# Kernel of four transformer layers: first attention as a pipeline over single tiles, ternary weights quantized inside the third layer's attention

## The chip, the cores and the metric

The kernel runs on one core of a Trainium2 chip. The metric is the device time of one execution in microseconds; the median of three runs is used. A core has the engines TensorE (PE, with its weight loads as PEld), VectorE (DVE), ScalarE (ACT), GpSimd (POOL) and SyncE (SP), which here only issues DMAs. Each engine runs its own list of instructions, and they meet at semaphores.

## What is computed

Four layers on 4096 tokens (64 sequences of 64) of width 256, float32. Each layer adds an attention and then a feed-forward part:

```
x = x + attention_l(layernorm(x), ctx, ...)
x = x + ffn_l(layernorm(x), ...)
```

The parts that the change touches are these. Layer 0's attention is over the 64 context rows of the same sequence, without projections, with a mask of keys:

```
scores  = xn @ ctx^T / 16, -1e30 where masked;  attn = softmax(scores)
out     = attn @ ctx, or 0 where a sequence has no valid key
```

Layer 0's feed-forward is a mixture of 32 experts (4 a token) and a shared expert, each `(silu(x w1) * (x w3)) w2`; layer 3's has 8 experts (2 a token) of width 176 and a shared one. Layer 1's feed-forward ("think") computes one vector for each sequence, from its last token, and adds `gate * vector` to each token before a layer norm. Layer 2's attention has 16 heads, a rotary part of the queries and keys, and weights that the kernel multiplies together beforehand. Layer 2's feed-forward is ternary:

```
quantize(w) = clip(round(w / (mean|w| + 1e-8)), -1, 1)
y = (silu(x Q(w1)^T) * (x Q(w2)^T)) Q(w3)^T          # w1, w2: 704 x 256, w3: 256 x 704
```

## The kernel before

x stays in SBUF (x_all) through the whole kernel, as 32 tiles of 128 tokens. The program is a row of stages, each with its own semaphores and buffers, which ends on all engines before the next begins. Between stages, finish_stats turns the mean and variance that each tile's last bn_stats left in bn_all into a mean and a reciprocal root, by three Newton steps on DVE (L195 to L210), and normalize (L219) uses them. The eight PSUM banks are c.bank[0] to c.bank[7].

stage_first loads x in four parts of eight tiles and takes their statistics (L262 to L271). stage_l0_attention then loads weights and masks, turns the masks into factors (keep, drop, any_valid, L454 to L456), and works in eight rounds of WIDE = 4 tiles. In a round each engine does each of its steps for four tiles before the next step. PE transposes xn and ctx (L226); makes key rows for the later layers' attentions (keys, L377, L380) and values and products with a Gram matrix (L384, L386) for them; makes the scores (L395); transposes prob (L401); and reads the context with it (L405). ACT copies out of PSUM and takes exponents (L441). DVE normalizes, multiplies the rotary key part with cosine and sine, scales and masks the scores and takes the maximum (L477 to L480), and adds the read to x with new statistics (L496, L498). POOL splits each context tile in three bfloat16 parts for layer 3 (L244 to L248), and adds the rotary products. SP loads a context tile to a slot when that slot's tile is done (x_done, L317), then stores the split parts (L324).

In the experts of layers 0 and 3, ACT takes the sigmoid of the gate half, DVE multiplies it with that half (L2942 in layer 3), and then by the other half to hid (L2944), which PE transposes.

In stage_l1_think tokens go in groups of four tiles. SP broadcasts each group's think rows from DRAM (L1321) into one of TH slots; POOL multiplies the gate with them (L1340) and does two more steps. After the second group's issue SP issues all seven weight loads for layer 2 (L1323 and following), some 4 MB, and the third group's rows come behind them. PE, ACT and DVE use these weights after their own last group.

stage_l2_attention works on two tiles in turn (LANES = 2, loops of pairs written with Fori). DVE's order for a tile is front (normalize, and a mask from three 64-wide operations, L1795 to L1798), maxima of the scores (L1818, L1820), sums of the exponents (L1825, L1826), rope of the next tile (L1809 to L1811, four times each), and back (L496, L498). POOL adds the rotated parts (L1667), PE makes queries (L1686), scores (L1721) and outputs (L1708).

stage_l2_ternary begins with a prelude in a block of its own: it loads the three raw weight matrices, takes their sums of absolute values (L1909 and its like), adds these over partitions by a matmul with ones, and quantizes each matrix with two comparisons and a subtraction (L1920 to L1922). Then come the tiles.

## Time and profile before

| | us |
|---|---|
| median of 3 runs | 2742.14 (2735.84 to 2747.07) |
| the profiled execution | 2754.47, span 2752.7 |
| load of x and its statistics | 0 to 22.0 |
| layer 0 attention | 22.4 to 225.1 |
| layer 0 experts (the last part) | 495 to 590 |
| layer 1 think | 777 to 954 |
| layer 2 attention | 959 to 1555 |
| quantization of the ternary weights | 1559.5 to 1586.6 |
| ternary feed-forward | 1587.2 to 1826 |
| layer 3 attention | 1832 to 2375 |
| layer 3 experts, with their gate | to 2752.7 |
| busy in the span: PE, DVE, POOL, ACT | 2011.5, 1745.9, 1170.6, 967.1 |

Times within the kernel are from the start of the profiled execution. In think, GpSimd's steps repeat every 8.3 us a group once the third has come (898.3, 905.9, 914.2, 922.5), and layer 2's precomputed weights follow on PE. In the rows of windows each engine's busy time has its number of instructions in brackets. "Idle before" in a row is the time that the engine stood still before the instruction, and "<-" names what released it. The granted clock is TensorE's as a share of full speed.

### The profile page before, as it was taken

Reading aid. Unit: us, or ns where it says so; the run is one execution under the profiler, and the core shown is the slowest. Engines: PE = TensorE matmul, PEld = TensorE weight load, DVE = VectorE, ACT = ScalarE, POOL = GpSimd, SP = SyncE. Lnnn points to the kernel's source line nnn. Section 1 sums busy time; section 2 is a strip of 40 time slices with the busy share of each in tenths; the row PEclk is TensorE's granted clock in tenths of the full one; section 3 lists DMA queues with packets and bytes.
Section 4 is the critical chain, followed back from the end, with each engine's and each line's share of the span. In section 5 each row is a group of like instructions: output and inputs, shape, how many; then the busy total and the mean of one; then the engine's idle time right before and its main releaser. Section 6 shows DMA issues by size and latency. Waiting matters only on the chain. (4 is left out here: it accounts for less than half of the span.)

```text
span 2752.7 us, 48931 instructions
## 1 busy us (share of the span) xinstructions
PE 2011.5 (73%) x17042; PEld 1511.4 (55%) x17074; DVE 1745.9 (63%) x3743; ACT 967.1 (35%) x2509; POOL 1170.6 (43%) x1482
## 2 busy tenths in 40 slices
PE   4776927536976077777777479959999999458995
PEld 3666826315855066666666356635666665135774
DVE  5554479324554878888888544457887885633446
ACT  2442201102423233333343122215666666222331
POOL 2430000462323745555555222335887887063331
PEclk9777965657988589999999789978999999778998
DMA  4224100561076100000000000024444441222336
GB/s 116 55 54 162 38 8 2 161 163 47 5 183 106 31 1 0 0 0 0 0 0 0 32 1 1 1 49 97 104 110 111 96 112 45 71 90 66 107 105 212
DMA packets 142050, 174.97 MB, mean 64 GB/s; under 512 B 30380, under 2 KB 123740, under 8 KB 137116
## 3 DMA queue, kind: packets, MB, share of 16 engines
q1 hardware_dynamic: 132044, 150.51, 20.7%
q0 software_dynamic: 9808, 21.93, 2.6%
q8 instruction: 110, 1.80, 0.3%
q14 instruction: 88, 0.72, 0.1%
HBM read 113.01 MB, written 58.79 MB: 62 GB/s over the span
## 5 line engine op out<-in xcount | busy, mean ns | idle before, releaser
L2512 DVE TENSOR_REDUCE mx<-bank 128x2 f32<-128x512 f32 x512 | 321.2, 680 | 91.4 <-PE bank L2374 91.3
L2478 ACT ACTIVATE e<-bank 128x512 f32<-128x512 f32 x512 | 269.1, 606 | 137.3 <-PE bank L2394 137.2
L2306 POOL TENSOR_TENSOR es<-e 128x256 f32<-128x256 f32 x384 | 271.0, 728 | 92.7 <-ACT e L2478 92.2
L2374 PE MATMUL bank<-k,q 72*128 72x256 bf16 x1024 | 203.7, 284 | 34.8 <-DMA k<-k_parts 34.8
L1667 POOL TENSOR_TENSOR q_l<-q_l,rot_l 64x1024 f32<-64x1024 f32 x64 | 150.5, 2352 | 182.0 <-DVE rot_l L1811 182.0
L2394 PE MATMUL bank<-q,k 74*128 74x256 bf16 x1024 | 195.5, 274 | 7.2 <-DMA q<-rows 4.7
L1708 PE MATMUL bank<-wvo,rd_l 128*128 128x256 f32 x512 | 120.6, 389 | 37.2 <-ACT rd_l L1766 37.2
L2374 PEld LDWEIGHTS bank<-k,q 72*128 72x128 bf16 x1024 | 92.1, 100 | 95.8 <-issue 51.6
L2411 PE MATMUL bank<-e,val 128*32 128x256 f32 x2048 | 140.5, 392 | 3.1 <-ACT nd L2473 0.6
L1686 PE MATMUL bank<-qcT,wq_abs 96*128 96x128 f32 x1024 | 125.0, 281 | 11.2 <-ACT qcT L1736 11.2
L1708 PEld LDWEIGHTS bank<-wvo,rd_l 128*128 128x128 f32 x512 | 95.7, 192 | 62.4 <-ACT rd_l L1766 50.4
L1686 PEld LDWEIGHTS bank<-qcT,wq_abs 96*128 96x128 f32 x1024 | 118.9, 195 | 18.3 <-ACT qcT L1736 18.3
L2836 POOL DMA_INDIRECT y<-y,got x71 | 69.0, 972 | 140.5 <-DVE y L2954 135.9
L2881 PE MATMUL bank<-w,hT 88*128 (+1 forms) x412 | 114.4, 403 | 19.2 <-issue 12.4
L1721 PE MATMUL bank<-key_l,q_l 128*64 128x64 f32 x2048 | 75.1, 227 | 59.4 <-POOL q_l L1667 37.7
L2394 PEld LDWEIGHTS bank<-q,k 74*128 74x128 bf16 x1024 | 97.2, 98 | 31.0 <-DMA q<-rows 9.8
L2942 DVE TENSOR_TENSOR sig<-bank,sig 128x176 f32<-128x176 f32 x103 | 35.1, 341 | 122.8 <-ACT sig L2901 66.6
L1721 PEld LDWEIGHTS bank<-key_l,q_l 128*64 128x64 f32 x2048 | 66.4, 140 | 76.2 <-POOL q_l L1667 42.1
L1809 DVE TENSOR_TENSOR q_l<-bank,const_sb 64x512 f32<-64x512 f32 x128 | 88.9, 695 | 21.6 <-PE bank L1686 19.7
L1652 POOL TENSOR_TENSOR sc_l<-sc_l,mx_l 128x512 f32<-128x512 f32 x64 | 66.7, 1042 | 77.6 <-DVE mx_l L1820 77.6
L1995 PE MATMUL bank<-w,rest_t 128*128 128x512 bf16 (+1 forms) x256 | 81.5, 318 | 23.6 <-DVEq L499 20.6
L2091 DVE TENSOR_TENSOR sig_t<-bank,sig_t 128x512 f32<-128x512 f32 x64 | 30.6, 520 | 106.4 <-ACT sig_t L2047 106.4
(455 smaller groups left out, 5308.2 us busy)
## 6 DMA issues: line engine op xcount, KB each, us to landing
q<-q_parts SPq DMA_DIRECT2D x32, 576.0 KB
k<-k_parts SPq DMA_DIRECT2D x96, 192.0 KB
got<-rows SPq DMA_DIRECT2D x71, 128.5 KB
rows<-no_row SPq DMA_DIRECT2D x1, 9088.0 KB, 43.9
moe_rows<-zero_b SPq DMA_DIRECT2D x16, 512.0 KB, 5.8
w<-in_e0w SPq DMA_DIRECT2D x16, 512.0 KB
moe_in<-moe_rows SPq DMA_DIRECT2D x16, 512.0 KB, 8.8
parts_y<-y SPq DMA_DIRECT2D x32, 256.0 KB, 4.6
```

Source lines behind the costliest of these rows:

```text
L1667: nc.gpsimd.tensor_tensor(q[64:P, j, hs, :], q[64:P, j, hs, :], rot[64:P, j, hs, :], ALU.add).then_inc(s["rope_added"], 1)
L1686: last = nc.tensor.matmul(bank(j, h // 4)[:, (h % 4) * P:(h % 4 + 1) * P], wq[:, h, :], qcT[:, j, :], start=True, stop=True)
L1708: last = nc.tensor.matmul(bank(j, 2)[:, 0:D], rd[:, j, hp, :], wvo[:, hp, :], start=(hp == 0), stop=(hp == HP - 1))
L1721: last = nc.tensor.matmul(bank(j, h // 8)[r, (h % 8) * S:(h % 8 + 1) * S], q[:, j, h, r], key[:, j, r], start=True, stop=True)
L1809: v.tensor_tensor(q[64:P, j, hs, :], raw[64:P], tab(c.cos, 64, P), ALU.mult)
L2306: nc.gpsimd.tensor_tensor(es[:, n, :], e[:, n, 0, :], e[:, n, 1, :], ALU.add).then_inc(s["sum_ready"], 1)
L2374: last = nc.tensor.matmul(scores(r)[:, qt * D:(qt + 1) * D], q[0:R, b, h * D + qt * P:h * D + qt * P + P], k[0:R, b, h * D:(h + 1) * D], s ...
L2394: last = nc.tensor.matmul(scoresT(r)[:, lt * D:(lt + 1) * D], k[:, b, h * D + lt * P:h * D + lt * P + P], q[:, b, h * D:(h + 1) * D], star ...
L2411: nc.tensor.matmul(readout[32 * r:32 * r + 32, 0:D], val[:, a.n % 2, r, i, lt, :], e[:, slot(i, r), lt, :], start=(i == 0 and lt == 0), st ...
L2478: nc.scalar.activation(e[:, slot(i, r), :, :].rearrange("p k n -> p (k n)"), scoresT(r)[:, :], ACT.Exp).then_inc(s["exp_ready"], 1)
L2512: v.tensor_reduce(mx[:, a.n, 0, at:at + 2], scores(r)[:, :].rearrange("p (a n) -> p a n", a=2), AX.X, ALU.max, negate=True).then_inc(s["ma ...
L2881: last = nc.tensor.matmul(out(u), hT[:, u % 2, n * P:(n + 1) * P], w, start=(n == 0), stop=(n == 1))
```

## The change

It has four parts.

1. stage_first and the first finish_stats go. The first attention loads x itself, and takes the statistics of the first eight tiles before its first normalization and those of the other 24 before that of tile 8. It is written out tile by tile: `steps` calls each engine's jobs at step n for tile n minus the job's lag, from three steps ahead (LEAD) to two behind. Context tiles have a ring of CTX = 6 slots. A second DMA brings each context tile transposed (in_ctx_cols, which the mix stage already uses), so that PE doesn't transpose it and ACT doesn't copy it. Rotary products are taken straight from PSUM. The masks become one array, drop, and the scores are scaled and masked in one operation.
2. In both experts ACT takes Silu in place of Sigmoid, and DVE's product falls away.
3. In think, layer 2's weights are issued in parts after groups 1 to 6. Some buffers moved into the array of raw weights.
4. The quantization moves into layer 2's attention: loads at its start, sums of absolute values before tile 12 on DVE, the scale after tile 13, and then one eighth of each matrix in each of the eight pairs that follow.

The diff, cut to its core:

```diff
+def newton_rstd(nc, c, link, src, mean, rstd, cols, eps):
+
+    v = nc.vector
+    m_even, m_odd = src[:, cols, 1], src[:, cols, 4]
+    v_even, v_odd = src[:, cols, 2], src[:, cols, 5]
+    mean, y = mean[:, cols], rstd[:, cols]
+    row = lambda n: c.small[:, n, cols]
...
-def stage_first(nc, c):
+def stage_l0_attention(nc, c):
+
 
     with ExitStack() as ctx:
-        CH = 4
-        s = open_sems(nc, ctx, "consts_loaded " + " ".join(f"x_loaded{n}" for n in range(CH)))
+        sb = lambda n, sh, dt=F32: ctx.enter_context(nc.sbuf_tensor(n, sh, dt))
+        CTX, LEAD, KR, R, CH = 6, 3, 4, 3, 4
+        PER = NT // CH
+        wh = sb("wh", [P, H1, P]); whT = sb("whT", [P, H1, P]); gram = sb("gram", [P, H1, P])
+        wkvcT = sb("wkvcT", [KVC, D]); wkr = sb("wkr", [KVC, R2]); wk = sb("wk", [P, DK, P])
+        mask8 = sb("mask8", [P, NT, S], U8); drop = sb("drop", [P, NT, S]); any_valid = sb("any_valid", [P, NT])
+        ctx_in = sb("ctx_in", [P, CTX, D]); ctxT = sb("ctxT_a", [P, CTX, DK, P])
+        xn = sb("xn_a", [P, R, D]); xT = sb("xT_a", [P, R, DK, P])
+        sc = sb("scores_a", [P, R, S]); prob = sb("prob_a", [P, R, P]); probT = sb("probT_a", [P, R, P])
+        nmax = sb("nmax_a", [P, NT]); tot = sb("tot_a", [P, NT]); rec = sb("rec_a", [P, NT])
+        rot = sb("rot_a", [P, R, 2, P])
+        k_rest = sb("k_rest", [P, KR, D]); k_parts = sb("k_parts_a", [P, KR, 3, D], BF16)
+        ctx_loaded = [f"ctx_loaded{n}" for n in range(CTX)]
+        k_stored = [f"k_stored{n}" for n in range(KR)]
+        x_loaded = [f"x_loaded{n}" for n in range(CH)]
+        s = open_sems(nc, ctx, "consts_loaded a_weights a_masks a_pre a_gram a_wk a_prob_zero a_chain a_split "
+                      "xn_ready feat_ready feat_copied v_ready v_copied keys_ready key_copied rot_ready keys_done "
+                      "scores_ready soft_ready prob_ready probT_ready probT_copied read_ready x_done k_low_ready "
+                      + " ".join(ctx_loaded + k_stored + x_loaded))
         block = ctx.enter_context(nc.Block())
-        xt = c.d["x"].rearrange("(n p) d -> p n d", p=P)
+        feat = c.bank[0][:, 0:D]
+        keys = lambda t: c.bank[1 + t % 2]
+        vg = lambda t: c.bank[3 + t % 2]
+        att = lambda t: c.bank[5 + t % 3]
+        x_rows = c.d["x"].rearrange("(n p) d -> p n d", p=P)
+
+        def wait(eng, sem, count):
+
+            if count > 0:
+                eng.wait_ge(s[sem], count)
+
+        def steps(*jobs):
+
+            for n in range(-LEAD, NT + 3):
+                for lag, job in jobs:
+                    if 0 <= n - lag < NT:
+                        job(n - lag)
 
         @block.sync
         def _(sp):
-            for n in range(CH):
-                sp.dma_start(c.x[:, 8 * n:8 * n + 8, :], xt[:, 8 * n:8 * n + 8, :]).then_inc(s[f"x_loaded{n}"], 16)
-            sp.dma_start(c.const[:, :], c.d["const"]).then_inc(s["consts_loaded"], 16)
-            sp.wait_ge(s["consts_loaded"], 16)
-
-        @block.vector
-        def _(dve):
-            for n in range(CH):
-                dve.wait_ge(s[f"x_loaded{n}"], 16)
-                for t in range(8 * n, 8 * n + 8):
...
+        CTX, LEAD, KR, R, CH = 6, 3, 4, 3, 4
+        PER = NT // CH
...
+        def steps(*jobs):
+
+            for n in range(-LEAD, NT + 3):
+                for lag, job in jobs:
+                    if 0 <= n - lag < NT:
+                        job(n - lag)
...
+            def load(t):
+                wait(sp, "read_ready", t + 1 - CTX)
+                wait(sp, "k_low_ready", t + 1 - CTX)
+                sp.dma_start(ctxT[:, t % CTX, :, :], c.d["ctx_cols"][t]).then_inc(s[ctx_loaded[t % CTX]], 16)
+                sp.dma_start(ctx_in[:, t % CTX, :], c.d["ctx"][t * P:(t + 1) * P, :]).then_inc(s[ctx_loaded[t % CTX]], 16)
+
+            def load_x(n):
+                rows = slice(PER * n, PER * n + PER)
+                sp.dma_start(c.x[:, rows, :], x_rows[:, rows, :]).then_inc(s[x_loaded[n]], 16)
+
+            def store(t):
+                sp.wait_ge(s["k_low_ready"], t + 1)
+                for a in range(3):
+                    sp.dma_start(c.k_parts[:, a, t * 2 * H3:(t + 1) * 2 * H3, :].rearrange("c h l -> h c l"),
+                                 k_parts[:, t % KR, a, :]).then_inc(s[k_stored[t % KR]], 16)
...
+            load(0)
             for b in range(2):
                 src = c.d["mask"].rearrange("(t b) k -> b t k", b=2)[b:b + 1].broadcast_to([64, NT, S // 4])
                 sp.dma_start(mask8[64 * b:64 * b + 64, :, :].bitcast(I32), src).then_inc(s["a_masks"], 16)
-            for i in range(0, NT // WIDE):
-                for j in range(WIDE):
-                    t = i * WIDE + j
-                    sp.wait_ge(s["x_done"], freed(t))
-                    sp.dma_start(ctx_in[:, j, :], ctx_d[bass.ds(t * P, P), :]).then_inc(s[f"ctx_loaded{j}"], 16)
-                for j in range(WIDE):
-                    t = i * WIDE + j
-                    sp.wait_ge(s["k_low_ready"], t + 1)
-                    settle(sp, s["sp_passed"])
-                    for a in range(3):
-                        sp.dma_start(c.k_parts[:, a, bass.ds(t * 2 * H3, 2 * H3), :].rearrange("c h l -> h c l"),
-                                     k_parts[:, j, a, :]).then_inc(s[f"k_stored{j}"], 16)
-            for j in range(WIDE):
-                sp.wait_ge(s[f"k_stored{j}"], 48 * (NT // WIDE) + 48)
+            for t in range(1, CTX):
+                load(t)
+            for n in range(1, CH):
+                load_x(n)
+            for t in range(NT):
+                store(t)
+                if t + CTX < NT:
+                    load(t + CTX)
...
+            steps((0, split), (-1, turn))
...
+            def key_rows(t):
+                pe.wait_ge(s[ctx_loaded[t % CTX]], 32 * (t // CTX) + 32)
+                wait(pe, "key_copied", t - 1)
+                wait(pe, "rot_ready", t - 1)
+                for k in range(DK):
...
+                    nc.tensor.matmul(keys(t)[:, 0:P], wk[:, k, :], ctxT[:, t % CTX, k, :],
...
+            steps((-1, features), (2, turn), (-LEAD, key_rows), (-LEAD, values), (2, read), (0, scores))
...
+            steps((2, turned_copy), (-1, feat_copy), (-LEAD, key_copy), (-LEAD, value_copy), (0, exponent))
...
+            def norm(t):
+                if t == 0:
+                    chunk_stats(0)
+                    newton_rstd(nc, c, ch.link, c.bn, c.mean, c.rstd, slice(0, PER), LN_EPS)
+                if t == PER:
+                    for n in range(1, CH):
+                        chunk_stats(n)
+                    newton_rstd(nc, c, ch.link, c.bn, c.mean, c.rstd, slice(PER, NT), LN_EPS)
+                wait(dve, "feat_ready", t + 1 - R)
+                normalize(nc, c, xn[:, t % R, :], t).then_inc(s["xn_ready"], 1)
...
+            def soften(t):
+                if t == 0:
+                    dve.wait_ge(s["a_masks"], 32)
+                    ch.link(v.tensor_copy(drop[:, :, :], mask8[:, :, :]))
+                    ch.link(v.tensor_reduce(any_valid[:, :], drop[:, :, :], AX.X, ALU.max))
+                    ch.link(v.tensor_scalar(drop[:, :, :], drop[:, :, :], 1.0, -NEG, ALU.subtract, ALU.mult))
+                dve.wait_ge(s["scores_ready"], t + 1)
+                wait(dve, "prob_ready", t + 1 - R)
+                ch.link(v.scalar_tensor_tensor(out=sc[:, t % R, :], in0=att(t)[:, 0:S], scalar=D ** -0.5,
+                                               in1=drop[:, t, :], op0=ALU.mult, op1=ALU.add))
+                v.tensor_reduce(nmax[:, t:t + 1], sc[:, t % R, :], AX.X, ALU.max, negate=True).then_inc(s["soft_ready"], 1)
...
+            steps((-2, norm), (-LEAD, rotate), (2, add), (0, soften))
...
-                v.tensor_tensor(sig[:, g % 2, :], gates(g)[:, 0:F0], sig[:, g % 2, :], ALU.mult).then_inc(s["e_chain"], 1)
-                dve.wait_ge(s["e_chain"], g + 1)
...
-                nc.scalar.activation(sig[:, u % 2, :], gates(u)[:, 0:HID3], ACT.Sigmoid).then_inc(s["sig_ready"], 1)
+                nc.scalar.activation(sig[:, u % 2, :], gates(u)[:, 0:HID3], ACT.Silu).then_inc(s["sig_ready"], 1)
...
+            ahead = [[], [(wuqT, c.d["wuqT"])], [(wukT, c.d["wukT"])], [(wqr, c.d["wqr"]), (c.seg_i[:, :], c.d["seg"])],
+                     [(wuvT, c.d["wuvT"]), (c.wdq[:, :, :], c.d["wdq"].rearrange("(k p) n -> p k n", p=P))],
+                     [(wo[:, quarter(0), :], c.d["wo2"][:, quarter(0), :]), (wo[:, quarter(1), :], c.d["wo2"][:, quarter(1), :])],
+                     [(wo[:, quarter(2), :], c.d["wo2"][:, quarter(2), :]), (wo[:, quarter(3), :], c.d["wo2"][:, quarter(3), :])]]
...
+        def run(eng, ahead, behind, after=lambda t, j: None, between=None):
+
+
+            def pair(i):
                 for j in range(2):
                     ahead(2 * i + j + 1, 1 - j)
                     behind(2 * i + j, j)
                     after(2 * i + j + 1, 1 - j)
+
+            ahead(0, 0)
+            after(0, 0)
+            with eng.Fori(0, FIRST_RUN) as i:
+                pair(i)
...
+            if between:
+                between()
+            with eng.Fori(FIRST_RUN, RUNS) as i:
+                pair(i)
...
+            def total():
+                pe.wait_ge(s["q_zero"], 2)
+                pe.wait_ge(s["q_sums"], 3)
+                nc.tensor.matmul(bank(0, 3)[:, 0:3], ones, abs_sums[:, :], start=True, stop=True).then_inc(s["q_total"], 1)
+                pe.wait_ge(s["q_seen"], 1)
+
+            run(pe, front, back, scores, total)
...
+            def magnitudes():
+                dve.wait_ge(s["q_loaded"], 64)
+                for n in range(2):
+                    v.tensor_reduce(abs_sums[:, n:n + 1], raw12[:, n, :], AX.X, ALU.add,
+                                    apply_absolute_value=True).then_inc(s["q_sums"], 1)
+                v.tensor_reduce(abs_sums[:, 2:3], raw3, AX.XY, ALU.add, apply_absolute_value=True).then_inc(s["q_sums"], 1)
+
+            def scales():
+                dve.wait_ge(s["q_total"], 1)
+                v.tensor_scalar(inv[:, :], bank(0, 3)[:, 0:3], 1.0 / (HID2 * D), EPS2, ALU.mult, ALU.add).then_inc(s["q_seen"], 1)
+                dve.wait_ge(s["q_seen"], 1)
+                qch.link(v.reciprocal(inv[:, :], inv[:, :]))
+
+            def quantize(n, i):
+                ch = Chain(dve, s["q_chain"], 1 + 9 * (i - FIRST_RUN) + 3 * n)
+                src = raw12[:, n, :] if n < 2 else raw3.rearrange("p a b -> p (a b)")
+                dst = c.w12[:, n, :] if n < 2 else c.w3[:, :, :].rearrange("p a b -> p (a b)")
+                w = (DK * HID2 if n < 2 else FT2 * D) // PIECES
+                at = bass.ds((i - FIRST_RUN) * w, w)
+                ch.link(v.tensor_scalar(below[:, 0:w], src[:, at], inv[:, n:n + 1], -0.5, ALU.mult, ALU.is_lt))
+                ch.link(v.tensor_scalar(src[:, at], src[:, at], inv[:, n:n + 1], 0.5, ALU.mult, ALU.is_gt))
+                ch.link(v.tensor_tensor(dst[:, at], src[:, at], below[:, 0:w], ALU.subtract))
...
-            with dve.Fori(0, NT // 2 - 1) as i:
+            with dve.Fori(0, FIRST_RUN - 1) as i:
                 step(2 * i, 0)
                 step(2 * i + 1, 1)
+            magnitudes()
+            step(2 * FIRST_RUN - 2, 0)
+            step(2 * FIRST_RUN - 1, 1)
+            scales()
+            with dve.Fori(FIRST_RUN, RUNS) as i:
+                step(2 * i, 0)
+                quantize(0, i)
+                step(2 * i + 1, 1)
+                quantize(1, i)
+                quantize(2, i)
...
-        with ExitStack() as pre:
-            wt = lambda n, sh: pre.enter_context(nc.sbuf_tensor(n, sh, F32))
-            raw12 = wt("raw12", [P, DK, 2, HW]); raw3 = wt("raw3", [P, FT2, D]); tmp = wt("tmp_q", [P, DK * 2 * HW])
...
-                for n in range(3):
-                    src = raw12[:, :, n, :] if n < 2 else raw3[:, :, :]
-                    dst = w12[:, :, n, :] if n < 2 else w3[:, :, :]
-                    a, b = (DK, HW) if n < 2 else (FT2, D)
-                    t3 = tmp[:, 0:a * b].rearrange("p (a b) -> p a b", a=a)
-                    ch.link(v.tensor_scalar(t3, src, inv[:, n:n + 1], -0.5, ALU.mult, ALU.is_lt))
-                    ch.link(v.tensor_scalar(src, src, inv[:, n:n + 1], 0.5, ALU.mult, ALU.is_gt))
-                    ch.link(v.tensor_tensor(dst, src, t3, ALU.subtract))
```

## Rows read from the trace of the kernel before

**Rows 1.** Windows: us; busy PE, PEld, DVE, ACT, POOL; granted clock; DMA share; GB/s

```profile
30.00:54.00 24.00, 14.47 (x120) 13.39 (x121) 14.04 (x40) 11.26 (x44) 11.10 (x20) 0.99 0.21 55
130.00:154.00 24.00, 18.10 (x124) 15.70 (x124) 13.41 (x45) 11.46 (x44) 9.68 (x21) 0.71 0.21 56
494.00:590.00 96.00, 52.98 (x241) 23.80 (x240) 19.20 (x60) 14.28 (x48) 56.94 (x45) 0.66 0.63 173
959.00:1300.00 341.00, 257.09 (x2447) 213.74 (x2448) 282.93 (x481) 129.30 (x299) 167.98 (x129) 0.97 0.00 0
```

**Rows 2.** Timeline of the start: start, duration (us), engine, line, operation, [idle before]

```profile
15.27 2.71 DVE L271 BATCH_NORM_STATS2 bn_all<-x_all 128x6 f32<-128x256 f32 x8 [0.27 <-DMA x_all<-in_x]
...
21.78 0.19 DVE L210 SCALAR_TENSOR_TENSOR rstd_all<-small,rstd_all 128x32 f32<-128x32 f32 x1
...
30.64 1.23 DVE L454 CAST keep<-mask 128x2048 f32<-128x2048 uint8 x1 [8.67 <-DMA mask<-in_mask]
...
33.12 2.27 DVE L456 TENSOR_REDUCE any_valid<-keep 128x32 f32<-128x2048 f32 x1
```

**Rows 3.** Timeline of one round of the first attention, and its last instruction

```profile
133.56 1.06 PE L377 MATMUL bank<-fT_a,wk 128*128 128x128 f32 x4
...
136.19 0.61 PE L377 MATMUL bank<-fT_a,wk 128*128 128x128 f32 x4
...
137.98 0.61 PE L377 MATMUL bank<-fT_a,wk 128*128 128x128 f32 x4
...
144.05 0.23 DVE L479 TENSOR_TENSOR scores_a<-scores_a,drop 128x64 f32<-128x64 f32 x1
...
147.76 3.78 PE L405 MATMUL bank<-ctx_in,probT_a 128*128 128x256 f32 x8
...
150.13 3.61 SPq L318 DMA_DIRECT2D ctx_in<-in_ctx  x4
...
152.41 0.40 POOL L244 COPY k_parts_a<-ctx_in 128x256 bf16<-128x256 bf16 x1 [9.51 <-DMA ctx_in<-in_ctx]
...
224.66 0.43 DVE L498 BATCH_NORM_STATS2 bn_all<-x_all 128x6 f32<-128x256 f32 x1
```

**Rows 4.** Single lines: minimum/median/maximum ns, first and last start

```profile
L219 DVE TENSOR_SCALAR xn_l<-x_all,mean_all,rstd_all x32: 415/1220/2551, 959.1 to 1517.5; 128x256 f32 x30, 128x256 f32<-128x256 f32 x2
...
L318 SPq DMA_DIRECT2D ctx_in<-in_ctx x32: 327/333/1368, 27.4 to 201.3; - x32
```

**Rows 5.** Timeline of the think stage, SyncE's issue and GpSimd

```profile
875.73 19.50 SPq L1321 DMA_DIRECT2D think<-think_rows  x6
...
891.35 2.77 POOL L1340 TENSOR_TENSOR gate_g<-gate_g,think 128x256 f32<-128x256 f32 x4 [11.34 <-DMA think<-think_rows]
```

**Rows 6.** Timeline of the third layer's attention, inside one tile

```profile
1390.88 2.35 POOL L1667 TENSOR_TENSOR q_l<-q_l,rot_l 64x1024 f32<-64x1024 f32 x1 [1.91 <-DVE rot_l L1811]
...
1393.99 0.20 DVE L1798 TENSOR_SCALAR drop_l<-drop_l 128x64 f32<-128x64 f32 x1
...
1400.17 0.69 DVE L1809 TENSOR_TENSOR q_l<-bank,const_sb 64x512 f32<-64x512 f32 x1 [0.29 <-PE bank L1686]
```

**Rows 7.** Timeline from the statistics before the ternary stage to its first tile

```profile
1558.82 0.19 DVE L210 SCALAR_TENSOR_TENSOR rstd_all<-small,rstd_all 128x32 f32<-128x32 f32 x1
...
1572.05 1.74 DVE L1909 TENSOR_REDUCE abs_sums<-raw 128x1 f32<-128x1536 f32 x1
...
1583.81 1.02 DVE L1921 TENSOR_SCALAR raw<-raw,inv_q 128x1536 f32<-128x1536 f32 x1
1584.86 1.76 DVE L1922 TENSOR_TENSOR w3q<-raw,tmp_q 128x1536 bf16<-128x1536 f32 x1
1587.20 0.74 DVE L219 TENSOR_SCALAR xn_t<-x_all,mean_all,rstd_all 128x256 f32<-128x256 f32 x2 [0.57 <-POOLq L162]
```

**Rows 8.** Last experts: a costliest group, and a wait (total us, times, longest)

```profile
L2942 DVE TENSOR_TENSOR sig<-bank,sig 128x176 f32<-128x176 f32 x103 | 35.1, 341 | 122.8 <-ACT sig L2901 66.6
...
PE bank L2867 <- DVE hid L2944: 4.9, 2, 3.6
```

424 lines of the change are left out of this document (171 added, 253 removed).

## Prediction

> **What bounds the kernel now.** I read the windows by stage first, then the timeline at both ends of each stage that the diff touches, then the waits. The span is a sequence of stages; each edit is worth what it moves in its own stage.
>
> The first attention does four tiles per round in 24.0 us, 6.0 a tile [rows 1], and no engine is full: PE 18.1, DVE 13.4, ACT 11.5, POOL 9.7 us. The engines take turns: reads at 147.76, the last add, then the four loads at 150.13, behind which POOL stood for 9.51 us until 152.41 [rows 3]. The granted clock is 0.71, against 0.99 in the first rounds: PE ran on both of its levels (1.2 and 2.4 GHz), seen as 1.06 and 0.61 us for the same four matmuls.
>
> In the third layer's attention DVE is busy 283 of 341 us, PE 257 at clock 0.97 [rows 1]. PE is followed closely: DVE's rotations start 0.29 us after it would be free [rows 6]. So DVE's order sets the period, 17.9 us a tile. The first layer's experts have POOL 57 of 96 us and a DMA share of 0.63; DVE has 19.
>
> The chain of waits agrees: in the think stage POOL stands 11.34 us for a think row block issued at 875.73 [rows 5]. The ternary stage opens with a prelude in which nothing else runs [rows 7].
>
> **Part 1, first attention.** Removed: the stage that loads x and takes the first statistics, and the statistics' own block, to 22.0 us [rows 2]. The new stage begins at zero, so its first read no longer waits for them; but masks (1.23, 1.30 by the cast's like and 2.27 us: 4.8) and 8 tiles' statistics (2.7) and the root (3.7: from 17.98, the statistics' end, to 21.97, less a block's start of 0.3) stand on DVE before the first softmax. Weights, x and five contexts now share one queue. I put the first normalized tile at 21.3 us and the first read at 36.
>
> Steady state. Per tile DVE has 13.41/4 = 3.35 us, less one 0.23 operation [rows 1, 3], about 3.5 with hand-overs; POOL 9.68/4 = 2.4; ACT 2.9. PE loses four transposes of context in eight and keeps about 2.9 at the high level, 5.8 at the low. If only engines counted, the period would be 3.5 us. But the ring of contexts has six slots, and a tile's context lives from its key rows, three steps ahead, to its read, two steps behind: six steps. The load of tile n+4 goes out only after the read of tile n-2 in step n, and its key rows are PE's next work but two. So each period holds a closed circle: key rows and values of a tile (1.79 us start to start, 136.19 to 137.98), the read (3.78/4 = 0.95 at clock 0.71, so 0.65 at the high level) [rows 3], the second load's issue (0.33 [rows 4]), the landing (2.28: 150.13 to 152.41 [rows 3]), and two semaphores, 0.3. Sum 5.35 us. SP's queue adds nothing: the three stores of a tile stand behind the load of the step before, need 2 us of issue (0.67 each, estimated from the 5.4 us of eight), and are through before the next read. At the low level PE's parts double: 3.6 + 1.3 + 0.33 + 2.28 + 0.3 = 7.8, take 7.7. These are the bounds of the period, beside 3.5 if the circle is not there.
>
> Which level? PE would work 2.9 of 5.35 us, 54%, with one gap of 2.3 us in each tile. Work at full speed (busy share times clock) and clock are 0.55 x 0.66 = 0.36 in the experts (0.66), 0.75 x 0.71 = 0.54 here (0.71), 0.75 x 0.97 = 0.73 in the third layer (0.97) [rows 1]. The new one has 0.54, as the old, but the old one's idle comes in stretches of up to 9 us and the new one's in gaps of 2.3. I take a clock of 0.80, a little above the nearest row: PE spends 60% of the time on the high level, and the period is 1/(0.6/5.35 + 0.4/7.7) = 6.1 us. The Trainium skill, "TensorE: Matmul & The Clock Gate", section "HAM oscillation — how this bites in real kernels", says that PE bursts separated by waits on DMA drop to the low clock each time; this change puts one such wait in every tile. No row here has this pattern at so short a beat. By it the sum would be that of the slow rival below.
>
> Sum: 36 + 26 periods of 6.1 (159) + the last five tiles without loads and the last add (20) + the other 24 tiles' statistics at step 6 (8.1 + 3.6 = 11.7 on DVE, of which ring slack takes about 4) 7.5 = 222, against 225.1 [rows 3]: **-3 us**. With 5.35: -23. With 7.7: +38. With 3.5: -71.
>
> **Part 2, Silu.** It removes a product per tile from DVE, 103 of 0.34 us in the last experts [rows 8] and 16 like them in the first. PE runs there without a break: it waited for DVE's hid 4.9 us in two times [rows 8]. The first experts are POOL's and the transfers' [rows 1]. The work that hides it is PE's own. One function table more could cost about a microsecond, on ACT, which idles. Value 0, range -3 to +1.5.
>
> **Part 3, think.** The L2 weights go out over six groups, wo in quarters, instead of all at one group ahead of the next think block. POOL's 11.34 us stop is that [rows 5], and behind it all stages ran at POOL's pace. The last quarters go at about 898 us; PE's precomputation with them, some 10 us, ends by 915, well ahead of the stage's end at 954. Value **-11**, range -12 to -4: each part of the weights now stands in SP's queue behind one think block and ahead of the next, for which POOL has its 8.3 us per group as cover; were a part longer than that, POOL would stop for the rest.
>
> **Part 4, quantization.** The prelude goes: from the end of the statistics, 1558.82 + 0.19, to 1587.20 less 0.54 for a block's start, **-27.6 us** [rows 7]. In it: the wait for DMA some 10, three reductions 5.2, nine operations (1.02 + 1.02 + 1.76) x 3 = 11.4. Their four loads are then under the attention, on a queue of SP's that is empty there (DMA share 0.00 [rows 1]), and the two memsets stand on POOL ahead of its first tile, under a microsecond.
>
> Added, on the engine that sets the period: a piece (compare, compare, subtract; 176 or 192 wide) three times in each of 8 pairs. No row has this width. Between 64 wide (0.20 compare [rows 6], 0.23 subtract [rows 3]) and 1536 wide (1.02, 1.76) lie about 0.26, 0.26, 0.35. The three are linked, and addressed by register, so gaps of 0.04 to 0.15 follow: a piece is 1.0 to 1.7, I take 1.33, nearer the narrow rows. Three pieces 4.0, plus 0.3; xn_l (median 1.22 against a smallest of 0.415, when POOL's q_l runs beside it [rows 4]) will be pushed behind q_l and lose some of that: -0.6. So 3.7 x 8 = 30 (22 to 40). Magnitudes are three reductions, of which the 1.74 row is one: 4.9, of which 1.1 falls into a wait, 3.8. Scales, the PE total in between and the wait for its bank: 2.2; one loop more on each engine: 1. Together +37 (28 to 48; below, if pieces fall into DVE's 17% idle). PE's wait for q_seen holds back its next front; it is in the 2.2. Net **+9** (0 to +20).
>
> **Sum.** -3 + 0 - 11 + 9 = -5 on the profiled execution's 2754.5. That one lies 0.45% over the median, so 2749.5 x 2742.1/2754.5 = **2737 us**.
>
> **Rivals.**
> *Clock stays high* (period 5.35): for it, gaps are short and the third layer kept 0.97 with 25% idle; against, 46% idle here. -25 in all: 2717.
> *The ring does not bind*, the first attention runs at DVE's pace, 3.5: if the landing is much shorter than 2.28 or PE finds its context landed. Against it is the order of slots. -73: 2669.
> *Quantization is hidden* in DVE's 58 us of idle in 341 [rows 1]: for it, idle exists in every tile, 3 us; against, it lies inside the chain (waits for ACT, links), behind which the added work does not slip. Part 4 is then -22: 2706.
> *Other side, TensorE falls to the low level* in the first attention and stays: period 7.7, +38 there, +36 in all: 2778, slower. It decides above a period of about 6.85 (26 x 0.75 = 19 us more than taken). For it: 0.66 to 0.71 in the two nearest rows; against: the old stage had the longer gaps. A lesser one is pieces at 1.7 with a chain that gives nothing back: +14.
>
> **How the numbers follow.** The forecast 0.39 (own range 2722 to 2752); clock high 0.17; ring not binding 0.10; quantization hidden 0.08; low clock 0.15; dear pieces 0.08; the rest unknown. A change of under 0.5%, 13.7 us, is about what a measurement of this kernel can't tell from none. The forecast's case holds a fifth that is faster by more. Faster 0.42, same 0.32, slower 0.26. Range: 2690 to 2775, leaving out the ring rival and the upper half of the low clock.
>
> **What would show it.** In the changed profile: PE's key rows stand for the context's DMA about 2.3 us in each tile, period 5.3 to 7.7 by the clock; the clock between 0.7 and 0.95 from 50 to 200 us. If PE never stands for it, the ring step is wrong. In think, POOL's stop of 11.34 is gone and the stage is shorter by as much. In the third layer's attention, the pairs after the seventh are 3.7 us longer, and between statistics and the ternary stage's first normalization lie under 1 us. The last experts' period stays at PE's. Wrong would be a period of the first attention outside 5.3 to 7.7, or pieces hidden.

## The result

The changed kernel took 2787.2 us in the median of four runs (2783.7 to 2793.4), the kernel before 2744.6: ratio 1.0154, interval 1.0120 to 1.0188. It is slower by 1.5%. The forecast was 2737 us, with a range of 2690 to 2775 and a chance of 0.26 for slower. The profiled execution took 2788.8 us (span 2787.0) against 2754.5.

The stages, each measured from where VectorE begins the statistics that follow the one to where it begins those that follow the next (for the first stage from zero), in the profiled executions:

| stretch | before | after | difference | forecast |
|---|---|---|---|---|
| load, statistics, first attention | 225.5 | 231.7 | +6.2 | -3 |
| shared expert, routing, experts, layer 0 | 412.5 | 413.7 | +1.2 | 0 |
| layer 1 attention | 134.9 | 133.9 | -1.0 | 0 |
| layer 1 think | 181.9 | 178.1 | -3.8 | -11 |
| layer 2 attention | 600.5 | 680.7 | +80.2 | +37 |
| ternary (before: with its prelude) | 272.3 | 243.8 | -28.5 | -27.6 |
| layer 3 attention | 517.2 | 514.8 | -2.4 | 0 |
| layer 3 gate, routing, experts | 407.9 | 390.3 | -17.6 | 0 |

Three of these need an explanation: 80.2 where 37 stood, the last stretch, and the think stage. The first attention also needs one: it came out 9 us above its forecast, by the mechanism that was forecast.

**First attention after.** The timeline of TensorE and SyncE over two tiles:

```profile
139.70 0.71 PE L364 MATMUL bank<-ctxT_a,wk 128*128 128x128 f32 x4 [1.66 <-DMA ctx_in<-in_ctx]
...
142.64 1.06 PE L396 MATMUL bank<-ctx_in,probT_a 128*128 128x256 f32 x2
...
143.74 0.33 SPq L295 DMA_DIRECT2D ctxT_a<-in_ctx_cols  x1
...
144.11 0.44 SPq L296 DMA_DIRECT2D ctx_in<-in_ctx  x1
...
146.31 0.71 PE L364 MATMUL bank<-ctxT_a,wk 128*128 128x128 f32 x4 [1.66 <-DMA ctx_in<-in_ctx]
...
153.54 0.74 PE L364 MATMUL bank<-ctxT_a,wk 128*128 128x128 f32 x4 [2.32 <-DMA ctx_in<-in_ctx]
```

The circle can be read off: key rows, read, the two loads issued as the read ends, the landing, the next key rows. TensorE stands in nearly every tile for a context. The waits from 70 us to the stage's end say so for all of it (us in total, times, longest):

```profile
PE bank L364 <- DMA ctx_in<-in_ctx: 35.2, 21, 2.3
```

A window of it shows the clock at 0.74, against 0.71 in [rows 1]; from 50 to 200 us it was 0.76:

```profile
135.00:159.00 24.00, 17.89 (x107) 14.08 (x105) 11.12 (x39) 7.93 (x32) 9.46 (x20) 0.74 0.23 61
```

**Layer 2's attention after.** VectorE's timeline behind one pair of tiles, with two pieces, and further down the rotations of the next tile; ahead of them GpSimd's q_l, which ends inside the first compare:

```profile
1287.20 2.35 POOL L1709 TENSOR_TENSOR q_l<-q_l,rot_l 64x1024 f32<-64x1024 f32 x1 [1.91 <-DVE rot_l L1859]
...
1288.79 0.87 DVE L1912 TENSOR_SCALAR raw_weights<-raw_weights,inv_q 128x176 f32 x1 [0.27 <-DVE bn_all L512]
1289.70 0.31 DVE L1913 TENSOR_SCALAR raw_weights<-raw_weights,inv_q  x1
1290.15 0.34 DVE L1914 TENSOR_TENSOR w<-raw_weights 128x176 f32 x1
1290.67 0.32 DVE L1912 TENSOR_SCALAR raw_weights<-raw_weights,inv_q 128x192 f32 x1 [0.17 <-DVE w L1914]
1291.02 0.32 DVE L1913 TENSOR_SCALAR raw_weights<-raw_weights,inv_q  x1
1291.48 0.36 DVE L1914 TENSOR_TENSOR w3q<-raw_weights 128x192 f32 x1
1292.66 0.41 DVE L225 TENSOR_SCALAR xn_l<-x_all,mean_all,rstd_all 128x256 f32 x1 [0.82 <-DVE w3q L1914]
...
1302.15 0.69 DVE L1857 TENSOR_TENSOR q_l<-bank,const_sb 64x512 f32<-64x512 f32 x1 [2.55 <-PE bank L1728]
```

The second piece, with GpSimd quiet, is 0.32 + 0.32 + 0.36 with its gaps, 1.2 us, near the 1.33 that was taken; the first, whose compare ran beside q_l, is 1.7. What stands beside them is the last row: VectorE waits 2.55 us for the query matmuls, where it waited 0.29 in [rows 6]. TensorE's timeline tells why; the tiles at 1314.81 and 1358.39 us follow a single piece:

```profile
1293.21 0.43 PE L232 MATMUL bank<-const_sb,xn_l 128*128 128x128 f32 x2 [2.44 <-DVE xn_l L225]
1294.10 1.17 PE L1722 MATMUL bank<-xT_l,wdq 128*96 128x128 f32 x4 [0.46 <-ACT xT_l L1781]
1295.62 6.38 PE L1728 MATMUL bank<-qcT,wq_abs 96*128 96x128 f32 x32 [0.35 <-ACT qcT L1784]
...
1314.81 0.44 PE L232 MATMUL bank<-const_sb,xn_l 128*128 128x128 f32 x2 [0.53 <-DVE xn_l L225]
1315.71 0.68 PE L1722 MATMUL bank<-xT_l,wdq 128*96 128x128 f32 x4 [0.46 <-ACT xT_l L1781]
1316.74 3.84 PE L1728 MATMUL bank<-qcT,wq_abs 96*128 96x128 f32 x32 [0.35 <-ACT qcT L1784]
...
1358.39 0.44 PE L232 MATMUL bank<-const_sb,xn_l 128*128 128x128 f32 x2 [0.53 <-DVE xn_l L225]
...
1360.81 6.21 PE L1728 MATMUL bank<-qcT,wq_abs 96*128 96x128 f32 x32 [0.35 <-ACT qcT L1784]
```

TensorE stood 2.44 us for the normalized tile, and the same 32 matmuls then took 6.38 us instead of 3.84: it was on its lower level for most of them. That happened behind all eight waits for a tile that follows two pieces (1.75 to 2.44 us), and behind five of the eight that follow one, though TensorE stands only 0.53 us there. The windows (columns as in [rows 1]) show the granted clock just behind the wait of 2.44 us and over the pairs with pieces. The third is of the loop of the kernel before: its clock was 1.00, and the 0.97 of [rows 1] came from the first 23 us of that window alone:

```profile
1290.00:1300.00 10.00, 6.74 (x53) 6.03 (x49) 6.85 (x17) 1.90 (x4) 3.60 (x5) 0.71 0.00 0
1300.00:1600.00 300.00, 222.63 (x1852) 188.62 (x1850) 232.91 (x414) 93.95 (x220) 125.16 (x95) 0.87 0.00 0
...
1000.00:1300.00 300.00, 231.91 (x2222) 192.16 (x2218) 255.20 (x436) 117.68 (x272) 153.11 (x117) 1.00 0.00 0
```

**Think after.** GpSimd's stop of 11.34 us [rows 5] is gone, as forecast:

```profile
893.30 3.51 POOL L1354 TENSOR_TENSOR gate_g<-gate_g,think 128x256 f32<-128x256 f32 x4 [0.20 <-DMA think<-think_rows]
```

But the thought vectors ahead of it, a part that the change only gave other buffers, were done 7 us later in this execution, with a clock of 0.83 (857 to 877 us) where it was 1.00 (850 to 870 us) before; over the stage's first 94 us it was 0.80 against 0.87.

### The profile page after: what moved, and what is told of

It is laid out like the page before. It is cut to its first block and busy times, and to the rows that moved or that the text cites. A ratio compares the mean times of both kernels' runs of the same rounds, so it can differ in the third digit from the quotient of the medians.

```text
span 2787.0 us, 48688 instructions
## 1 busy us (share of the span) xinstructions
PE 2076.6 (75%) x16978; PEld 1567.4 (56%) x17010; DVE 1714.0 (61%) x3673; ACT 953.6 (34%) x2479; POOL 1172.1 (42%) x1480
## 5 line engine op out<-in xcount | busy, mean ns | idle before, releaser
L1728 PE MATMUL bank<-qcT,wq_abs 96*128 96x128 f32 x1024 | 168.2, 341 | 11.2 <-ACT qcT L1784 11.2
L1728 PEld LDWEIGHTS bank<-qcT,wq_abs 96*128 96x128 f32 x1024 | 162.0, 253 | 20.2 <-ACT qcT L1784 20.2
L2971 DVE TENSOR_TENSOR hid<-bank,sig 128x176 f32<-128x176 f32 x103 | 35.2, 342 | 105.0 <-ACT sig L2930 104.9
L2889 PE MATMUL bank<-w,xT 128*128 x284 | 95.7, 459 | 0.0
```

The source lines that it names most:

```text
L1728: last = nc.tensor.matmul(bank(j, h // 4)[:, (h % 4) * P:(h % 4 + 1) * P], wq[:, h, :], qcT[:, j, :], start=True, stop=True)
L2889: last = nc.tensor.matmul(gates(u)[:, 0:2 * HID3], src(k), w(k), start=(k == 0), stop=(k == DK - 1))
```

## The experiments

Kernels of one group ran on one chip, those of the second and third on the same one at different times; ratios are to the kernel before in the same group, with 95% intervals. Stage times are those of the table above.

**First group: which part is it?** The prelude put back (layer 2's attention and ternary stage as before):

> The changed kernel with the quantization put back in its prelude between layer 2's attention and the ternary tiles (part 4 undone, the other three parts kept). Theory: the loss is in part 4 and is 80.2 us in the attention less 28.5 us in the prelude, 52 us; then this kernel takes 2787 - 52 = 2735 us, a little faster than the kernel before, and the attention's pairs fall back to 35.8 us with a granted clock of 0.97 or so. Rival: the first attention, whose ring keeps TensorE waiting, leaves the clock low for what follows; then the attention of layer 2 keeps 20 us or more of its loss and the kernel stays above 2755 us.

Measured: ratio 0.9994 (0.9967 to 1.0022). The attention took 602.1 us and the ternary stretch 272.1, as before. The loss is part 4's; the first attention leaves no trace of 20 us or more in layer 2's attention. The kernel came out even with before (2756.6 us, before 2759.1 on this chip) and not 10 us under it; that number was made with a last stretch of 390.3 us, which was 408.7 here.

Eight context slots:

```diff
-        CTX, LEAD, KR, R, CH = 6, 3, 4, 3, 4
+        CTX, LEAD, KR, R, CH = 8, 3, 4, 3, 4
```

> The changed kernel with eight slots for contexts (CTX = 8) in the first attention, nothing else. Theory: the circle of key rows, read, issue and landing sets the first attention's period, 6.9 us at the clock that it got; with two slots more the load goes out two steps earlier, PE does not wait for it, and the period falls to that of the busiest engine, 3.5 to 4.5 us: the stage ends at 150 to 175 us instead of 231, and the kernel takes 2705 to 2735 us. Rival: the period is held by TensorE at its low level or by the hand-overs between the engines; then it falls by under 1 us and the kernel takes 2765 us or more.

Measured: ratio 1.0010 (0.9990 to 1.0030), some 1.4% under the changed kernel's 1.0154. The stage ended at 188.2 us instead of 231.7, and not at the 150 to 175 that were expected. The period fell from 6.3 to 4.5 us, and the wait for a context is gone from TensorE's waits. The total lies above my range of 2705 to 2735 (2760.8 on a chip where before took 2759.1). The theory had the cause right and the size too large: 43.5 us in the stage where it said 56 or more, since something else holds the period at 4.5 (the last run below shows what). The clock rose by itself:

```profile
102.00:126.00 24.00, 17.42 (x151) 14.28 (x150) 15.59 (x54) 11.61 (x53) 12.40 (x26) 1.00 0.40 104
```

Sigmoid and VectorE's product put back:

> The changed kernel with Sigmoid and DVE's product back in both experts (part 2 undone). The last stages, from layer 3's statistics on, took 390.3 us against 407.9 before, which I had put at nothing. Theory: the gain is Silu's, since DVE and ACT stand in a chain with the scattered rows while the shared expert runs; then this kernel is 10 to 18 us slower than the changed one, 2797 to 2805 us, and the stretch takes 400 us or more. Rival: the difference is chance in that stretch (ScalarE stood 9.9 us once before for nothing that the profile shows); then the kernel stays within 5 us of 2787.

Measured: ratio 1.0162 (1.0110 to 1.0214), as the changed kernel's 1.0154; the last stretch took 409.0 us. The time alone, 2808.9 us, looks like the theory, but the kernel before was 14.5 us slower on this chip as well. With the 408.7 us of the kernel with the prelude back, which has Silu, this spoke for chance; a run with Silu alone stands below.

The pieces left out, everything else of part 4 kept. The kernel thus leaves out the quantization itself; GpSimd sets the two weight arrays to zero instead (not shown in the diff):

```diff
                 step(2 * i, 0)
-                quantize(0, i)
                 step(2 * i + 1, 1)
-                quantize(1, i)
-                quantize(2, i)
```

> The changed kernel without the 24 pieces of the quantization: loads, sums of absolute values, the scale and the split loops stay, the ternary weights are zero instead. It leaves out the quantization itself. The eight pairs with pieces took 43.9 us each, 8.1 more than before, where the pieces' own instructions on DVE are some 4.5 to 5. Theory: the rest, some 3 us, is TensorE's clock: the gap that a piece makes lets it fall (0.71 in 1290 to 1300 us), and its query matmuls then come late to the rotations; without pieces the pairs are 35.8 us and the clock is 0.97 again, and the kernel is 65 us faster, 2722 us. Rival: the clock falls for another reason (the loads, the second loop, the state that the stage begins in); then the pairs stay above 37.5 us, the clock under 0.93, and the kernel is under 50 us faster.

Measured: ratio 0.9925 (0.9903 to 0.9948), the attention 611.8 us, its pairs 35.83 us, and the clock of the pairs full:

```profile
1280.00:1540.00 260.00, 201.16 (x1959) 166.94 (x1956) 221.73 (x379) 99.97 (x230) 132.72 (x103) 1.00 0.00 0
```

So loads, sums, scale and loops cost 11.3 us of the 80.2, and the pieces 68.9 at most. Some 4 of these are not theirs: the first three tiles took 58 us here and 63.9 in the changed kernel, with a clock of 0.53 from 975 to 995 us, and the kernels with eight slots and with the shorter lead, which have the same pieces and began in 58 us, took 676.9 and 677.0 us. Measured against those two the pieces cost 65. The kernel was 2.3% faster than the changed one, as expected.

**Second group: is it the clock?** Identity matmuls on TensorE ahead of its wait behind two pieces, only in the second loop (`warm` is filled between the loops, which the diff leaves out):

```diff
             def front(t, j):
+                if warm and j == 1:
+                    for _ in range(20):
+                        nc.tensor.matmul(bank(1, 3)[:, 0:P], c.ident, c.ident, start=True, stop=True)
                 pe.wait_ge(s["xn_ready"], ready(t))
```

> The changed kernel with 20 matmuls of the identity (128 columns, no one reads the result) on TensorE ahead of its wait for the normalized tile that comes behind two pieces, in the second loop of layer 2's attention only. It adds work and takes none away. Theory: the pieces cost twice, 4.5 us a pair on VectorE's order and 3.5 to 4 us because TensorE stands 2.44 us, falls to its low level, and takes 6.4 us instead of 3.8 for the query matmuls. With the gap filled the clock stays at 1.00 in the pairs and they take 40 to 41 us in place of 43.9; the kernel is 25 to 30 us faster than the changed one, 10 to 20 us above before. Rival: the filled time is as long as what it saves, or VectorE's order alone sets the pair; then the pairs stay at 43 us or more.

The same in the first attention, 14 ahead of the wait for a context, and then 8. The edit also moves that wait behind the two others:

```diff
-                pe.wait_ge(s[ctx_loaded[t % CTX]], 32 * (t // CTX) + 32)
                 wait(pe, "key_copied", t - 1)
                 wait(pe, "rot_ready", t - 1)
+                for _ in range(14 if t >= CTX else 0):
+                    nc.tensor.matmul(keys(t)[:, D:D + P], c.ident, c.ident, start=True, stop=True)
+                pe.wait_ge(s[ctx_loaded[t % CTX]], 32 * (t // CTX) + 32)
```

> The changed kernel with 14 matmuls of the identity ahead of TensorE's wait for a context in the first attention, from tile 6 on; the ring keeps its six slots. Theory: my circle's formula holds, 5.35 us at the high level and 7.7 at the low; with TensorE kept busy the clock stays at 1.00, the period falls from 6.9 to 5.4 to 5.7, and the stage ends at 190 to 198 us in place of 231.7. Rival: the clock falls all the same, or the added matmuls lengthen the circle by more; then the stage ends later than 215 us.

Measured: ratio 1.0166 (1.0122 to 1.0209), the stage's end at 231.7, no change, and so a miss: the clock was 1.00, but 28 records took 3.29 us and made nearly every period of the key rows 6.21.

> As the kernel with 14 identity matmuls ahead of the wait for a context, but with 8, since 14 took 3.2 us and were themselves the circle (6.2 us a tile at clock 1.00). Theory: 8 take 1.8 us, under the wait of 2.3, so the circle is again the context's, 5.35 us at clock 1.00; the stage ends at 195 us or so. Rival: the stage stays beyond 215 us, and the period is not made of the terms that I named.

Measured: ratio 1.0080 (1.0052 to 1.0108). TensorE at clock 1.00 has only a rest of its wait left, and the period is 5.36 us in the mean of 19 tiles (5.35 forecast for the high level):

```profile
148.83 0.71 PE L366 MATMUL bank<-ctxT_a,wk 128*128 128x128 f32 x4 [0.57 <-DMA ctx_in<-in_ctx]
...
154.12 0.71 PE L366 MATMUL bank<-ctxT_a,wk 128*128 128x128 f32 x4 [0.15 <-DMA ctx_in<-in_ctx]
```

The stage ended at 206.8 us, not at 195; the theory's bound of 215 is kept, its number is not. The match of the mean is partly luck: the context's wait was over 0.2 us in nine tiles only (0.28 to 1.33 us, periods of 5.4 to 6.5), and where it was under 0.1 us the 16 added records stood in its place (periods of 5.0 to 5.2).

The same pieces, but one of the two in the middle of the step:

```diff
                 for n in range(2):
                     maxima(t, j, n)
+                middle()
                 for n in range(2):
                     sums(t, j, n)
...
-                step(2 * i + 1, 1)
-                quantize(1, i)
+                step(2 * i + 1, 1, lambda: quantize(1, i))
                 quantize(2, i)
```

> The changed kernel with the second piece of each pair moved from the end of the step to between the maxima and the sums, where VectorE stood 0.5 us for ScalarE; the same instructions in all. Theory: a wait of TensorE for the next normalized tile of 0.5 us a tile leaves the clock up, as it did behind the single piece; pairs of 40 to 41 us, the kernel 25 us faster than the changed one. Rival: a piece in the middle delays the sums and with them TensorE's transposes, so that TensorE stands elsewhere; pairs stay above 42.5.

Measured: ratio 1.0090 (1.0062 to 1.0118), the attention 653.1 us, pairs of 40.85. With no work added or removed, 27.6 us less in the attention, 23.8 beside 676.9; by the ratios the kernel gained some 18 us, not 25, which the intervals leave open. The pairs are as expected, but not for the reason given: the clock did not stay up. TensorE stands 1.1 us behind the piece at the step's end and 0.53 behind the other tile's, fell behind both in nearly every pair, and took some 5.47 us for the queries:

```profile
1350.40 0.44 PE L232 MATMUL bank<-const_sb,xn_l 128*128 128x128 f32 x2 [0.54 <-DVE xn_l L225]
...
1352.33 5.46 PE L1728 MATMUL bank<-qcT,wq_abs 96*128 96x128 f32 x32 [0.35 <-ACT qcT L1784]
...
1285.00:1580.00 295.00, 223.24 (x1968) 188.34 (x1964) 249.01 (x441) 97.57 (x228) 132.69 (x102) 0.92 0.00 0
```

What fell are two of VectorE's waits over the pairs. That for the queries was 29.4 us in the changed kernel (1268 to 1600 us) and is 10.8 here (1285 to 1580), since TensorE starts them earlier and is on the low level for a shorter time. That for ScalarE ahead of the sums went from 13.4 to 6.8, since the moved piece lies in it; that part has nothing to do with the clock:

```profile
DVE q_l L1857 <- PE bank L1728: 10.8, 13, 2.1
DVE sm_l L1873 <- ACT sc_l L1789: 6.8, 15, 0.6
```

The other place for the arithmetic: loads under the attention, the sums of absolute values on VectorE ahead of the last tile's output, the rest in whole matrices behind it, with eight context slots.

> The changed kernel with eight context slots, and with the quantization's loads under layer 2's attention but its arithmetic not in the loop: the sums of absolute values in VectorE's wait ahead of the last tile's output, the rest in whole matrices at the attention's end. Theory: the attention loses nothing in its loop (600 to 605 us), and what is left of the prelude is 12 to 14 us of nine wide operations and the scale; so from layer 2's statistics to the ternary stage's it takes 14 to 20 us less than before. With the ring's 40 us and the think stage's 11, the kernel is 60 to 75 us faster than before. Rival: parts fight each other through the clock, and less than 45 us is left.

Measured: ratio 0.9780 (0.9743 to 0.9817), 2682.4 us against 2742.9. This version beats both kernels. Its attention loop has pairs of 35.8 us again; with the arithmetic the stage takes 617.3 us and the ternary stretch 244.4, together 11.1 us less than before, a little under my 14 to 20; its first three tiles took 63.9 us, as the changed kernel's, where before they took 57.4, and that start is 6 us of what is missing. The 60.5 us between the medians lie at the lower edge of the 60 to 75. The sums lie in a wait, as the timeline of its end shows:

```profile
1505.96 3.09 DVE L1892 TENSOR_REDUCE abs_sums<-raw_weights 128x1 f32<-128x1408 f32 x2
1508.97 1.74 DVE L1894 TENSOR_REDUCE abs_sums<-raw_weights 128x1 f32<-128x1536 f32 x1
1516.67 0.42 DVE L510 SCALAR_TENSOR_TENSOR x_all<-bank,x_all 128x256 f32<-128x256 f32 x1 [5.96 <-PE bank L1746]
```

**Third group, the rest.** Silu alone on the kernel before:

> The kernel before with Silu for Sigmoid and without VectorE's product in both experts (part 2 alone). The stretch from layer 3's statistics after its attention to the end took 407.9 us before and 409.0 in the changed kernel with Sigmoid, but 390 to 409 in seven kernels with Silu. Theory: Silu shortens that stretch when the scattered rows and the shared expert run together, by 10 us or so, and the kernel is 0.2 to 0.6% faster than before. Rival: nothing on the path, ratio within 0.2% of 1, and the stretch is 400 us or more.

Measured: ratio 1.0008 (0.9993 to 1.0024), the last stretch 406.4 us. The theory falls: Silu is worth nothing here. The stretch took 390 to 393 us in the changed kernel and in all four of the second group, and 401 to 409 us in the seven kernels with Silu of the other groups; it goes with the group and not with the kernel. The kernel before, which has Sigmoid, shows the same in its medians: 2744.6 and 2742.9 us where the stretch was short, 2759.1 and 2756.9 where it was long, the 2742.9 and the 2756.9 on the same chip.

Six slots and a shorter lead:

```diff
-        CTX, LEAD, KR, R, CH = 6, 3, 4, 3, 4
+        CTX, LEAD, KR, R, CH = 6, 2, 4, 3, 4
```

> The changed kernel with LEAD = 2 and the ring of six kept: key rows and values are made two steps ahead instead of three, so a context lives five steps in six slots. Theory: one step of slack is enough, since the landing of 2.3 us is shorter than a period; the stage ends at 185 to 200 us as with eight slots, with no more memory, and the kernel is about 1.4% faster than the changed one. Rival: a shorter lead makes TensorE wait for ScalarE's and VectorE's work on the keys, and the stage ends beyond 215 us.

Measured: ratio 0.9979 (0.9964 to 0.9995), 1.7% under the changed kernel, where 1.4% was expected. The stage ended at 181.5 us, even below the 185 to 200, and but for the statistics' one nearly every period was 4.59 or 4.60. What now holds it is a circle of two engines. ScalarE's list goes from the exponent through the copies of probT and xT to those of the keys; VectorE waits for these keys, rotates them, adds the read, takes statistics, and then scales the next scores and takes their maximum, for which ScalarE's next exponent waits (rows of the timeline; the last line is ScalarE's wait from 70 to 170 us: total, times, longest):

```profile
121.99 0.35 ACT L439 ACTIVATE prob_a<-scores_a,nmax_a 64x64 f32<-64x64 f32 x1 [2.34 <-DVE nmax_a L493]
...
123.73 0.29 DVE L478 TENSOR_TENSOR rot_a<-bank,const_sb 64x128 f32<-64x128 f32 x1 [1.46 <-ACT keysT L426]
...
126.33 0.22 DVE L493 TENSOR_REDUCE nmax_a<-scores_a 128x1 f32<-128x64 f32 x1
...
126.58 0.35 ACT L439 ACTIVATE prob_a<-scores_a,nmax_a 64x64 f32<-64x64 f32 x1 [2.34 <-DVE nmax_a L493]
...
ACT prob_a L439 <- DVE nmax_a L493: 51.6, 22, 2.4
```

From exponent to exponent it is 4.59 us, 1.7 on ScalarE and 2.8 on VectorE, with no wait for TensorE in it. The same two waits, 2.2 to 2.4 and 1.46 us, stand in the kernel with eight slots.

## Why the prediction was wrong

**The step that failed** is the sum of part 4: "So 3.7 x 8 = 30 (22 to 40)". The pieces cost 65 to 69 us. They were costed on VectorE's order alone, and two things were off.

*The wait that they hand on to TensorE changes its clock.* The prediction looked at the granted clock in the first attention and took layer 2's attention at its 0.97 as given. Behind two pieces TensorE stood 2.44 us, fell to its low level and did the queries in 6.38 instead of 3.84 us, on which VectorE then waited. Filling that wait with useless matmuls took 29 us off, 25.5 of them beside a kernel whose stage began as well; that is the clock's share as far as a run shows it alone. Moving one piece took 27.6 off, 23.8 by the same measure, of which some 7 are VectorE's wait for ScalarE that the piece now fills. Neither run is free of the low level, which also came behind single pieces, so the clock's whole share was not measured; it is probably larger than 25.5. The Trainium skill, "TensorE: Matmul & The Clock Gate", section "HAM oscillation — how this bites in real kernels", says that matmul bursts separated by waits for a DMA drop to the low clock each time. I weighed it where the wait was for a DMA and not where it was for VectorE. This trace agrees where the wait was 1.75 to 2.44 us for VectorE; behind the waits for a DMA in the first attention the clock went up and down about its 0.76, and did not stay low.

*The pieces themselves*, with what is left of the clock in them, cost at most 651.4 - 611.8 = 39.6 us by the filled wait and 653.1 - 611.8 = 41.3 by the moved piece, about 5 a pair, against 30 and an upper end of 40. The estimate of 1.33 us was right for a quiet piece (1.2 us). But the first compare of a tile took 0.87 to 1.24 us beside GpSimd's q_l; that contention I had seen on xn_l, and booked as a saving of 0.6 a pair. xn_l did fall to 0.41 us, but the contention moved to the piece instead.

*Sums, scale and loops* cost 11.3 us; 7 was forecast. Together with the prelude's -28.5 (forecast -27.6), part 4 is +51.7 us and not +9. That alone takes the result out of the range.

**First attention**: the mechanism was right. The ring holds it: eight slots or a shorter lead take 43 to 50 us off. With the clock held at 1.00 by added matmuls the period was 5.36 us in the mean (5.35), in part by luck as said above. In the changed kernel the clock was 0.76 where 0.80 was taken, so the period was 6.3 us in the mean and not 6.1. The first addition came at 41.1 us, where the first read was forecast for 36. The second statistics made their period 15.0 us, 8.7 more than another, of which the two short periods behind it (4.59 us) gave back 3.4: 5.3 where 7.5 was taken. 222 forecast, 231.4 measured. The rival of a low clock is halfway right, and that of a ring that does not bind is refuted. Its floor was wrong too: without the ring the period is 4.5 to 4.6 and not the 3.5 that I had from counting each engine's work, since ScalarE and VectorE wait for each other in their fixed orders.

**Think**: the step was right in mechanism and size. The stop went from 11.34 to 0.20 us. Eleven other profiled kernels with this part took 169.7 to 176.1 us for the stage, the kernel before 181.9 and the one with Silu alone 183.0. The profile of the changed kernel hides it behind a later start, for which the lower clock ahead of the stop speaks: the three other kernels whose thought vectors came over 2 us late had 0.80 to 0.84 in the stage's first 94 us as well.

**Silu**: right, nothing. Its price shows too: ScalarE loads a function table ten times instead of eight, at 1.28 us each, and the ratio of 1.0008 shows no gain to set against it. The -17.6 us of the last stretch belong to the execution and not to the change, and where they come from stays open. It may also be why the profiled executions differ by 34 us and the medians by 43; no trace of a short execution of the kernel before is there to show it.

The rival on the other side was the first attention at the low level. The kernel did end on that side, but through the same clock in a stage where I had not asked about it.

## What to carry to other kernels

When work is put in an engine's gaps, ask whose wait it lengthens, and if that is TensorE's, price the low clock behind the wait, not only the wait. Two small insertions at one place cost some 24 us more here than the same two at two places, of which some 7 came from a wait that the moved one filled. In a ring, count from the earliest step that fills a slot to the last that reads it: a life of as many steps as there are slots puts the whole load latency into each period, and one step less of lead mends it without memory. Work that does not fit into a full loop may still have its loads there, and its arithmetic in the waits at the loop's end.

## What the runs showed of the hardware

In a loop where TensorE was busy three quarters of the time and stood 1.16 and 1.20 us in each tile, the clock was 1.00 throughout (kernel before, 1000 to 1300 us). One more wait in the tile was enough to lose it: behind 1.75 to 2.44 us it fell eight times of eight, and behind 0.53 us five times of eight (changed kernel, queries of 5.5 to 6.2 instead of 3.84 us). With one piece moved it fell behind 1.1 us and behind 0.53 us in nearly every pair. In the first attention with eight slots it kept 1.00 from 72 to 170 us with 1.2 us of waiting in 4.5. So the length of the last wait alone does not tell it. Useless matmuls in a wait made a kernel faster (attention 680.7 to 651.4 us). A 176-wide compare took 0.31 us alone and 0.87 to 1.24 beside a GpSimd tensor operation.
